# Graph-layer kernel: inner results kept in PSUM, the diagonal term on VectorE, the digraph biases opened by three row groups, and a new planned order

## The reference

```python
x = _layernorm(x + L0(x, adj))   # attention of 12 heads, q, k, v with biases, masked by adj > 0
x = _layernorm(x + L1(x, adj))   # 2 times: exp(h W h^T) * adj, times (h W_lin^T + b), norm, relu
x = _layernorm(x + L2(x, adj))   # 2 times the digraph layer below
x = _layernorm(x + L3(x, adj))   # attention of 12 heads with adj as bias, output projection
# a digraph layer of L2:
a = softmax(h h^T / temper); delta = a * adj; attn = delta / (sum(delta) + 1e-10)
ctx = (attn * upper) @ (h wl^T + bl) + diag(attn) * (h ws^T + bs) + (attn * lower) @ (h wr^T + br)
h = relu(layernorm(ctx) * g + beta)
```

## Time and profile before

| | us |
|---|---|
| median of 3 runs | 2933.51 |
| lowest, highest | 2930.34, 2935.92 |
| the profiled execution's own time | 2933.42 |
| its span, first to last instruction | 2931.7 |
| PE busy, in 35008 matmuls | 2823.5 |
| DVE busy | 2403.6 |
| ACT busy | 1825.3 |
| POOL busy | 1349.7 |

### The profile page before, as it was taken

The page is one execution under the profiler, slowest core; times in us unless marked ns, Lnnn a source line. Parts: engine busy times, 40 slices in busy tenths (PEclk is TensorE's granted clock), DMA queues, the critical chain, the costliest instruction groups (busy, mean ns, idle before and its releaser), DMA issues.

```text
span 2931.7 us, 93395 instructions
## 1 busy us (share of the span) xinstructions
PE 2823.5 (96%) x35008; PEld 2091.8 (71%) x35008; DVE 2403.6 (82%) x8566; ACT 1825.3 (62%) x4885; POOL 1349.7 (46%) x2571
## 2 busy tenths in 40 slices
PE   6899999999999999999999999999999999999996
PEld 4666767777777777777777777777777777777764
DVE  6867888788888888888888888888888878888767
ACT  5745566566666666666666666666666666665546
POOL 2334454354454454454454454454454445444545
PEclk9899999999999999999999999999999999999997
DMA  9414354344444444444454454444443444544325
GB/s 238 86 30 72 67 101 77 61 84 70 84 86 68 84 85 72 83 86 69 84 84 71 84 84 71 85 84 70 85 84 70 82 77 80 91 79 75 56 39 101
DMA packets 803991, 237.41 MB, mean 81 GB/s; under 512 B 771544, under 2 KB 803416, under 8 KB 803424
## 3 DMA queue, kind: packets, MB, share of 16 engines
q1 hardware_dynamic: 795808, 218.28, 42.3%
q10 hardware_dynamic: 7744, 13.17, 1.4%
HBM read 29.99 MB, written 12.58 MB: 15 GB/s over the span
## 4 chain that ended last, share of the span: by engine, by line
PE 76%; DMA 7%; DVE 6%; ACT 3%; POOL 3%; SPq 2%; issue 2%; ACTq 0%; DVEq 0%; POOLq 0%
PE bank L801 10%; PE bank L802 9%; PE bank L803 9%; PE bank L789 8%; PE bank L790 7%; PE bank L791 7%; PE bank L893 6%; DMA turned<-flat 6%; PE bank L838 4%; PE bank L807 3%; PE bank L886 2%; PE bank L823 2%; PE bank L825 2%; PE bank L824 2%; DVE score L974 2%
## 5 line engine op out<-in xcount | busy, mean ns | idle before, releaser
L789 PE MATMUL bank<-turned,w_hi 128*128 128x128 f16 x4608 | 817.2, 220 | 19.7 <-DMA turned<-flat 17.7
L790 PE MATMUL bank<-turned,w_hi 128*128 128x128 f16 x4608 | 816.4, 220 | 0.0
L791 PE MATMUL bank<-turned,w_lo 128*128 128x128 f16 x4608 | 816.3, 220 | 0.0
L801 PE MATMUL bank<-w_hi,turned 128*128 128x384 f16 x2112 | 692.4, 328 | 23.7 <-DVE w_lo L925 14.2
L802 PE MATMUL bank<-w_lo,turned 128*128 128x384 f16 x2112 | 691.0, 327 | 0.0
L803 PE MATMUL bank<-w_hi,turned 128*128 128x384 f16 x2112 | 690.8, 327 | 0.0
L716 ACT ACTIVATE score<-score,small 128x128 f32<-128x128 f32 x1536 | 500.9, 391 | 152.7 <-DVE small L980 138.0
L707 ACT ACTIVATE ab<-bank 128x384 f16<-128x384 f32 (+1 forms) x768 | 367.0, 484 | 254.3 <-PE bank L791 130.8
L609 POOL TENSOR_TENSOR flat<-score,flat 128x384 f16<-128x384 f32 x256 | 237.2, 927 | 613.6 <-ACT flat L722 613.0
L789 PEld LDWEIGHTS bank<-turned,w_hi 128*128 128x128 f16 x4608 | 453.8, 98 | 51.8 <-DMA turned<-flat 22.4
L790 PEld LDWEIGHTS bank<-turned,w_hi 128*128 128x128 f16 x4608 | 453.9, 99 | 18.6 <-issue 13.1
(11 more groups left out here) (116 smaller groups left out, 6559.0 us busy)
## 6 DMA issues: line engine op xcount, KB each, us to landing
turned<-flat SPq DMA_TRANSPOSE x960, 2.8
x<-x_dram SPq DMA_DIRECT2D x64, 192.0 KB, 2.4
out_dram<-score SPq DMA_DIRECT2D x64, 192.0 KB, 2.2
w_stage<-w_dram ACTq DMA_DIRECT2D x19, 576.0 KB, 5.6
adj<-adj_dram SPq DMA_DIRECT2D x64, 64.0 KB, 2.3
rows<-rows_dram ACTq DMA_DIRECT2D x1, 1920.0 KB, 9.3
turned<-bias_dram SPq DMA_DIRECT2D x4, 9.0 KB
beta<-beta_dram SPq DMA_DIRECT2D x1, 0.5 KB, 6.3
```

The lines of the kernel that those rows point to most:

```text
L789: pe.matmul(dst, lhsT=w_hi[:, w, k, cols], rhs=t_hi[u][:, k, :], start=(k == 0), stop=False)
L790: pe.matmul(dst, lhsT=w_hi[:, w, k, cols], rhs=t_lo[u][:, k, :], start=False, stop=False)
L791: last = pe.matmul(dst, lhsT=w_lo[:, w, k, cols], rhs=t_hi[u][:, k, :], start=False, stop=(k == DT - 1 and w not in BIAS_OF))
L801: pe.matmul(dst, lhsT=t_hi[u][:, k, :], rhs=w_hi[:, w, k, :], start=(k == 0), stop=False)
```

## The change

1. `inner` and `gain` write their 384 columns in place in the PSUM bank of `mix` (`inner_of`), and `turn` and `residual` read them there. `e` stays in the banks of `u_gcn` and `u_di` (`e_of`). The banks are given back by the last of these readers.
2. In the digraph layers `mix` is two products, not three. The diagonal of delta is reduced to one column on DVE in `turn_delta`, and a new DVE instruction in `inner` adds the self projection times this column. The mask of three becomes one of two. (The triangle constants are reordered for it.)
3. A new PE step `open` writes the three biases of a digraph layer to three banks, each by a matmul of 32 rows in a row group of its own; the nine matmuls of each of the three projections then add to it.
4. POOL `sums` is two operations; two TICK copies are gone; `divide` waits for whichever of its four ACT copies comes last in the order.
5. The table of steps has new wanted and taken times; transposes are planned to land after 3.60 us; the plan models the DMA queue and a cold PE; weights 6 to 18 are loaded only after a named step of unit 0 (`LOADED_AFTER`). Every engine's order and every bank is therefore laid out anew.

```diff
-PERIOD = 43.452
...
+PERIOD = 43.087
...
+ARRIVES = {("load", 0): 2.20, ("load", 1): 2.90, ("load", 2): 4.50, ("load", 3): 6.10, ("load", 4): 7.70, ("load", 5): 9.30, ("load", 6): 10.90, ("weight", 0): 6.60, ("weight", 1): 9.10, ("weight", 2): 11.60, ("beta", 0): 9.00, ("bias", 0): 8.00}
+LOADED_AFTER = {6: ((SCALAR, "scores", 1),), 7: ((SCALAR, "scores", 2),), 8: ((SCALAR, "scores", 3),), 9: ((SCALAR, "turn", 1),), 10: ((SCALAR, "project", 3),), 11: ((SCALAR, "project", 4),), 12: ((SCALAR, "u_gcn", 0),), 13: ((SCALAR, "turn", 2),), 14: ((SCALAR, "project", 6),), 15: ((SCALAR, "norm", 1),), 16: ((SCALAR, "turn", 3),), 17: ((SCALAR, "u_di", 0),), 18: ((SCALAR, "turn", 4),)}
...
-    (PE, "mix", 2): (502.90, 2.010, 2.240, ((VECTOR, "turn_delta", 0), (SCALAR, "project", 9), (SCALAR, "project", 10), (SCALAR, "project", 11)), ()),
+    (PE, "mix", 2): (319.959, 1.340, 1.570, ((VECTOR, "turn_delta", 0), (SCALAR, "project", 9), (SCALAR, "project", 10), (SCALAR, "project", 11)), ()),
+    (PE, "open", 0): (277.841, 0.250, 0.250, ((SYNC, "turn", 3),), ()),
-    (VECTOR, "inner", 2): (450.45, 1.370, 1.565, ((PE, "mix", 2),), ()),
+    (VECTOR, "inner", 2): (308.293, 1.901, 2.323, ((PE, "mix", 2),), ()),
-    (SYNC, "turn", 0): (288.41, 1.240, 3.150, ((POOL, "turn", 0),), ()),
+    (SYNC, "turn", 0): (194.888, 1.240, 3.600, ((POOL, "turn", 0),), ()),
...
+        ONCE[SCALAR, "load_weight", n] = (FIRST + n - STAGES + 0.4, 0.0, 0.5, 5.2, ((VECTOR, "weight", WEIGHT_ORDER[n - STAGES]), *LOADED_AFTER.get(n, ())))
...
+TRANSFER = {(SYNC, "turn"): 1.25, (SYNC, "scores"): 1.25, (SYNC, "load"): 0.95, (SYNC, "store"): 0.7,
+            (SCALAR, "load_weight"): 1.85, (SCALAR, "load_rows"): 6.2}
+QUEUED, FIRST_WEIGHTS = 1.1, 5.5
+COLD_AFTER, COLD = 2.5, 1.7
+READ_BY = {"project": lambda w, n: (SCALAR if w in (5, 8, *range(9, 15)) else VECTOR, "project", w) if w != L3_O else (VECTOR, "residual", 3),
+           "scores": lambda s, n: (VECTOR, "scores", s), "attend": lambda s, n: (SCALAR, "attend", s),
+           "open": lambda k, n: (SCALAR, "project", L2_W[k][n]),
+           "turn_adj": lambda k, n: (SCALAR, "turn_adj", k), "u_gcn": lambda k, n: (VECTOR, "delta_gcn", k),
+           "u_di": lambda k, n: (VECTOR, "delta_di", k), "turn_delta": lambda k, n: (VECTOR, "turn_delta", k),
+           "mix": lambda k, n: ((VECTOR, "turn", 2), (VECTOR, "residual", 1), (VECTOR, "turn", 4), (VECTOR, "residual", 2))[k]}
+def banks_of(name, k):
+    if name == "project" and w_is_opened(k):
+        return 0
+    return 3 if name in ("scores", "open") else 1
+def w_is_opened(w):
+    return w in (*L2_W[0], *L2_W[1])
...
-            able = [max(t, free[engine], freed[BANKS_OF.get(part[1], 1) - 1][0] if engine == PE else 0.0)
+            able = [max(t, free[engine], freed[banks_of(*part[1:]) - 1][0] if engine == PE and banks_of(*part[1:]) else 0.0)
...
-        if part in TRANSPOSES and now < CROWDED:
-            until += 1.0
+        if part[:2] in TRANSFER:
+            until += max(0.0, queues_free - (now + QUEUED))
+            queues_free = max(now + QUEUED, queues_free) + TRANSFER[part[:2]]
+            if (part, i) == ((SYNC, "load", 0), 0):
+                queues_free += FIRST_WEIGHTS
+        if engine == PE:
+            if now - last_busy > COLD_AFTER:
+                busy, until = busy + min(busy, COLD), until + min(busy, COLD)
+            last_busy = now + busy
         free[engine] = now + busy
...
         delta = [a[:, N:2 * N] for a in score_at]
-        delta3 = score
-        o = zc = out = score_at
-        small = per_unit("small", [128, 4 * H + 6 + 2 + 13])
...
+            if name == "project" and w_is_opened(k):
+                name, k, n = "open", (k - L2_W[0][0]) // 3, (k - L2_W[0][0]) % 3
             return pool_of_banks[BANKS_AT[name, k, i][0][n]]
+        def e_of(i, name, layer):
+            return bank(name, layer, i)[:, 0:N]
+        def inner_of(i, k):
+            return bank("mix", k, i)[:, 0:D]
...
-            "inner": ("inner st", "sum", "inner mv", "centred") if k < 2 else ("inner st", "inner mv", "centred"),
+            "inner": ("inner st", "sum", "inner mv", "centred") if k < 2 else ("summed", "inner st", "inner mv", "centred"),
+            "turn_delta": ("diagonal",),
             "gain": ("gain base", "gain") if k < 2 else ()}.get(name, ()))
...
-                def step(what, dst, a, b, op):
-                    pool.tensor_tensor(col(u, dst), a, b, op).then_inc(gpsimd_done.of(i), 1)
-                    pool.wait_ge(*gpsimd_done.at(i, what, layer))
                 pool.wait_ge(*mixed_out.at(i, "delta_di", layer))
-                step("part of sum", DENOM, col(u, ZSUM), constant(DEN_EPS), ALU.mult)
-                step("sum", DENOM, col(u, DENOM), col(u, DSUM), ALU.add)
-                step("sum squared", DENOM, col(u, DENOM), col(u, DENOM), ALU.mult)
-                pool.tensor_tensor(col(u, EPS), col(u, DENOM), constant(INNER_EPS), ALU.mult).then_inc(gpsimd_done.of(i), 1)
+                pool.tensor_scalar(col(u, DENOM), col(u, ZSUM), 1e-10, col(u, DSUM), ALU.mult, ALU.add).then_inc(gpsimd_done.of(i), 1)
+                pool.wait_ge(*gpsimd_done.at(i, "sum", layer))
+                pool.tensor_scalar(col(u, EPS), col(u, DENOM), col(u, DENOM), 1e-12, ALU.mult, ALU.mult).then_inc(gpsimd_done.of(i), 1)
             def inner(i, k):
...
-                act.activation(flat[u][:, 0, :], src[u], ACT.Relu if k in (2, 4) else ACT.Copy).then_inc(cast.of(i), 1)
+                if k in (2, 4):
+                    act.activation(flat[u][:, 0, :], inner_of(i, k - 2), ACT.Relu).then_inc(cast.of(i), 1)
+                else:
+                    act.activation(flat[u][:, 0, :], src[u], ACT.Copy).then_inc(cast.of(i), 1)
...
-                act.activation(e[u], e[u], ACT.Exp).then_inc(scalar_done.of(i), 1)
+                act.activation(e_of(i, "u_gcn", layer), e_of(i, "u_gcn", layer), ACT.Exp).then_inc(scalar_done.of(i), 1)
             def u_di(i, layer):
                 u = i % UNITS
                 act.wait_ge(*mixed_out.at(i, "bias of u", layer))
-                act.activation(e[u], bank("u_di", layer, i)[:, 0:N], ACT.Exp, bias=col(u, UBIAS), scale=1.0 / TEMPER, accum_out=col(u, ZSUM))\
+                act.activation(e_of(i, "u_di", layer), e_of(i, "u_di", layer), ACT.Exp, bias=col(u, UBIAS), scale=1.0 / TEMPER, accum_out=col(u, ZSUM))\
...
-                    elif read_by == "u_gcn":
-                        pe.wait_ge(*numbers.at(j, "masked", n))
-                    elif read_by == "u_di":
-                        pe.wait_ge(*scalar_done.at(j, "e_di", n))
+                    elif read_by in ("delta_gcn", "delta_di"):
+                        pe.wait_ge(*mixed_out.at(j, read_by, n))
+                    elif read_by == "turn":
+                        pe.wait_ge(*mixed_out.at(j, "low x", n))
                     elif read_by == "turn_delta":
                         pe.wait_ge(*mixed_out.at(j, "delta3", n))
-                    elif read_by == "inner":
-                        pe.wait_ge(*numbers.at(j, "centred", n))
                     else:
                         pe.wait_ge(*mixed_out.at(j, "added", n))
...
             def project_natural(u, w, made):
-                dst = made[:, 0:D]
+                dst, opened = made[:, 0:D], w_is_opened(w)
                 for k in range(DT):
-                    pe.matmul(dst, lhsT=t_hi[u][:, k, :], rhs=w_hi[:, w, k, :], start=(k == 0), stop=False)
+                    pe.matmul(dst, lhsT=t_hi[u][:, k, :], rhs=w_hi[:, w, k, :], start=(k == 0 and not opened), stop=False)
                     pe.matmul(dst, lhsT=t_hi[u][:, k, :], rhs=w_lo[:, w, k, :], start=False, stop=False)
                     last = pe.matmul(dst, lhsT=t_lo[u][:, k, :], rhs=w_hi[:, w, k, :], start=False,
-                                     stop=(k == DT - 1 and w not in BIAS_OF))
-                if w in BIAS_OF:
+                                     stop=(k == DT - 1 and (opened or w not in BIAS_OF)))
+                if w in BIAS_OF and not opened:
                     bias, picked = bias_of(w)
                     last = pe.matmul(dst, lhsT=picked, rhs=bias, start=False, stop=True)
                 return last
+            def biases_are_made():
+                pe.wait_ge(bias_made, 2)
+                pe.wait_ge(picks_made, 3)
+            def open_banks(i, k):
+                if (k, i) == first(PE, "open"):
+                    biases_are_made()
+                bank_is_read(i, "open", k)
+                for n, w in enumerate(L2_W[k]):
+                    group = slice(HD * (BIAS_OF[w] % HG), HD * (BIAS_OF[w] % HG) + HD)
+                    pe.matmul(bank("open", k, i, n)[:, 0:D], lhsT=pick[group, BIAS_OF[w] % HG, :],
+                              rhs=bias_rows[group, BIAS_OF[w] // HG, :], start=True, stop=False)
             def project(i, w):
                 if (w, i) == first(PE, "project", w):
                     pe.wait_ge(w_lo_made, PLACE[w] + 1)
```

(36 more changed lines are left out.)

420 lines of the change are left out of this document (207 added, 213 removed).

## The result

The changed kernel takes 2890.86 us (median of four runs, 2887.13 to 2896.24); the kernel before, on the same chip, 2934.72 us (2930.34 to 2939.37). The ratio is 0.9852, with a 95% interval from 0.9828 to 0.9875: 43 us faster, where 92 were forecast. The sign was right and the range held the time, but more than half of the gain that was worked out did not come.

What follows compares the result with a forecast made beforehand. PE, busy 96% of the span, was taken as the full engine. The sum 2931.7 - 82.8 - 26.9 - 8 - 5 + 30 = 2839.0 us of span gave 2841 us, within about 2810 to 2868; the wider range was 2802 to 2900.

Steps and rivals of the forecast that it cites:

- third product off PE, less the new waits: In `mix` of two digraph layers: one product fewer saves 82.8 us of PE; new PE waits cost 30 us.
- biases: On PE: two `open` steps at 0.27 us replace six bias matmuls at 0.16 us a unit, saving 26.9 us in all.
- landings and weights on demand: PE's waits for transposes shrink by 8 us (0 to 17); late weight loads gain 5 us in the first 100 us.
- PSUM residence with banks held longer: On DVE, line 1064 reading PSUM saves 0.82 us a unit; longer-held banks are a source of the +30 us waits.
- The order: New engine orders: later planned transposes save 8 us and weights on demand 5 us.
- VectorE's balance of +0.96 us a unit: DVE's added and saved work sums to 38.7 us a unit; its whole addition as PE waits would be 61 us.
- Banks ran out: Rival: ten steps a unit take three banks at once, each waiting 0.15 us, 96 us in all: 2907; chance 12%.
- VectorE's work as PE's wait in full: Rival: DVE's added work becomes PE's wait in full, 61 in place of 30 us: 2872; chance 10%.
- VectorE did not take over: Rival: DVE takes over with its 6.5 us idle a unit unshrunk, 45.2 us a unit, 64 us more: 2997; chance 5%.
- the row groups don't overlap: Rival: row groups of `open`'s bias matmuls on PE don't overlap at 384 columns: 2868; chance 5%.

Runs made afterwards that it cites:

- e6: Changed kernel with three products in `mix` and three masks again, the diagonal's DVE instruction dropped, orders and banks kept: 2932.75 us, 0.9989 of before.
- e4: Changed kernel with the three bias matmuls of `open` as 128-row matmuls one after the other: 2896.85 us, 0.9863 of before.
- e5: Changed kernel with each bias added by a 128-row matmul behind its projection, `open` only taking its banks: 2896.74 us, 0.9869 of before.
- e11: Old work of PE and VectorE, with old bank releases, on the changed kernel's orders and late weight loads: 2944.86 us, 1.0029 of before.
- e1: Changed kernel with the masks step moved about 12 us later in VectorE's order: 2863.13 us, 0.9750 of before.
- e13: Changed kernel with three products and three masks again, no diagonal instruction, and the masks moved later in VectorE's order: 2937.37 us, 1.0014 of before.
- e14: Changed kernel with each group of three 32-row bias matmuls issued twice, the second time adding: 2902.56 us, 0.9893 of before.
- e8: Changed kernel with e, centred value and z in SBUF and their banks given back as before the change: 2892.23 us, 0.9841 of before.
- e7: Changed kernel with e, centred value and z back in SBUF, banks taken and given back as in the changed kernel: 2894.38 us, 0.9861 of before.
- e9: Changed kernel with the masks one step later in VectorE's order, behind the layer norm of `mix` 2, units 18 to 52: 2871.57 us, 0.9785 of before.

## Why the prediction fell short

By its own steps, the pieces measured as differences of ratios, times 2934 us:

| step | forecast | measured |
|---|---|---|
| third product off PE, less the new waits | -82.8 + 30 = -53 | -40 (after against e6) |
| biases | -26.9 | -3 to -5 (e4, e5) |
| landings and weights on demand | -8 - 5 = -13 | +8.5 (e11 against before) |
| PSUM residence with banks held longer | in the waits | -7 to -9 (what e11 to e6, -11.7, has beyond the biases) |

They add up to -43. The intervals leave 4 to 10 us on each line, most on the biases; that line and the last can't be told apart well, as no run changes one of them on the old work.

**The order: the step that failed, 21 us and more.** I took a quarter off the waits for landings and 5 us off the first 100 us, and gave the new order no price of its own. The gains are there with the old work: in e11 PE is idle for 13 us less up to 2000 us. (In the changed kernel the waits for landings fall from 17.7, 17.1, 8.5 and 1.8 us at four lines to 1.5, 21.3, 9.7 and 4.5, 8 us in all.) But the same order costs 12 us in the last stretch and 11 us for f32 products behind `scores` steps, and together that is the +8.5. It has a third price that shows only beside the diagonal: it puts the masks next to POOL's two instructions and ahead of the diagonal, and moving them away gives 28 to 30 us back (e1), and nothing without the diagonal (e13 against e6). Why the new orders drain worse is not settled: no run changed the last units alone.

**The biases: a term mis-sized, 12 us in PE's work and about 20 in the time.** The forecast 0.27 us from a group's start to the next step is what the timeline shows, but in part by luck. The 0.27 us of the `scores` row is three passes of 128 columns, its starts spread over 0.13 us, and 0.15 us to come out; I scaled it by columns, and an `open` is one pass of 0.16 us and 0.10 us more to come out. What I set against it was wrong as well: a step's price is what it adds between its two neighbours, and the 0.10 us ahead of the group was not in my sum. With 0.37 us the term is 0.97 - 0.73 = 0.24 us a unit, 15 us, and of that the waits took back a part (e5). The Trainium skill's rule (TensorE: Matmul & The Clock Gate, Measured speedup vs the span model) that a pack of row tiles takes one matmul and some 4 ns for each further tile holds for what lies inside the pack: 3 to 4 ns between the starts in e14, one pass for three. It leaves out the two changes of form around it, and these are half of the price, 0.20 of 0.37 us.

**The third product and the waits: right mechanism, place wrong, 13 us.** PE's own saving is confirmed by e13 to e1, 1.25 us of period against 1.29. Of that, 0.62 us of period is left in the changed kernel (e6 to after), so the waits took back 0.67 us a unit where I took 0.47; added idle time on the page is 36 us, the drain's share included. I had bounded them by VectorE's balance of +0.96 us a unit, and the balance came out near +0.6 (37.7 to 38.3; 36.8 in e1, where the masks are short). A sum over the unit did not tell what mattered: one stretch, in which the diagonal (0.61 us) stands behind two masks that had grown by 1.2 us. The prediction looked for contention only at the lines that the change edits, and not at those that a new order would put beside POOL's instructions. By the Trainium skill (SBUF — State Buffer, SBUF: two separate sides) VectorE and GpSimd share a port pair as an exclusive lock, so that the loser waits for a whole instruction. The timeline agrees: each mask ends 0.08 and 0.15 us behind its POOL instruction, at 3.6 and 2.8 times its own length.

**The rivals.** Banks ran out (12%, 2907) is nearest in time, and holds of 8 us did become a wait at a three-bank step, `scores` 7, as e8's period shows (0.50 us a unit); but one such step waits, not ten, and from e7 to e8 the time falls by 2 us (6 by the ratios), within the intervals. VectorE's work as PE's wait in full (10%) names the right engine. VectorE did not take over: it is busy for 85% of the span, and its idle time shrank from 6.5 to 5.1 us a unit. That the row groups don't overlap is refuted by e14.

**A version that beats both** is e1, the changed kernel with the masks moved: 2863.13 us (2857.45 to 2867.16), 0.9750 of before.

## What to carry to other kernels

Price a step by the distance between its neighbours with and without it, in the timeline; a change of matmul form has a price before and behind that no record carries. When an order is laid out anew, ask which VectorE instructions on SBUF will now run beside GpSimd's, and what stands behind them in that stretch: here moving the masks by one place in 35 of 64 units (e9) was worth 19 us, nearly half of the whole change. And run the old work on a new order before crediting the order with anything, or blaming an edit for what the order brought.
